# A new order of tile work in a fused shift-and-binary-convolution stage, with three of four sign pieces on GpSimd

## The reference

```python
x = x + shift(_gn(x))       # layer 0: offsets dy, dx (0 to 28) from the mean features; the image moved by them, zeros outside
x = x + conv3x3(sign(_gn(x)), sum of sign(W)) + b      # layer 1: SAME padding
x = x + spectral(_gn(x))    # layer 2: DCT along y, DFT along x, 32 x 32 modes mixed, back, relu with a 1x1 product
x = x + spectral(_gn(x))    # layer 3: the same with other weights
```

## Time and profile before

| | us |
|---|---|
| median of 3 runs | 4056.27 |
| the profiled execution, its own time | 4058.18 |
| its span, first to last instruction | 4056.4 |
| the first stage, until the last piece of its spectrum is copied | about 2203 |
| first `add_conv` of image 1 to that of image 14 | 1702.3 (13 periods of 130.9) |
| busy in the span: PE, DVE, ACT, POOL | 3117.6 (77%), 2755.7 (68%), 1483.0 (37%), 36.9 (1%) |
| bytes moved, mean rate | 808.65 MB, 199 GB/s |

### The profile page before, as it was taken

The page is one execution under the profiler, slowest core; times in us unless marked ns, Lnnn a source line. Parts: engine busy times, 40 slices in busy tenths (PEclk is TensorE's granted clock), DMA queues, the critical chain, the costliest instruction groups (busy, mean ns, idle before and its releaser), DMA issues. The chain is left out here.

```text
span 4056.4 us, 58465 instructions
## 1 busy us (share of the span) xinstructions
PE 3117.6 (77%) x17264; PEld 1421.0 (35%) x17264; DVE 2755.7 (68%) x3864; ACT 1483.0 (37%) x2708; POOL 36.9 (1%) x23
## 2 busy tenths in 40 slices
PE   0277877787877877778786579988998964799997
PEld 0133333333333333233333533333333324344443
DVE  3777665766577656766651557777677744599998
ACT  3455653655455544565433422222222214000000
POOL 0000000000000000000000000000000001000000
PEclk9987886888788877788887589999999976799998
DMA  4666544654466445655433475655665516799998
GB/s 144 176 183 199 160 155 130 203 169 150 131 188 203 141 130 163 203 160 155 139 111 107 93 293 213 251 214 205 240 247 201 219 61 125 270 379 387 390 385 305
DMA packets 272195, 808.65 MB, mean 199 GB/s; under 512 B 85466, under 2 KB 119774, under 8 KB 261108
## 3 DMA queue, kind: packets, MB, share of 16 engines
q1 hardware_dynamic: 212948, 488.15, 37.9%
q10 hardware_dynamic: 58368, 316.72, 20.3%
q0 software_dynamic: 608, 0.63, 0.1%
HBM read 479.39 MB, written 329.56 MB: 199 GB/s over the span
## 5 line engine op out<-in xcount | busy, mean ns | idle before, releaser
L817 DVE SCALAR_TENSOR_TENSOR A_image<-A_cps,A_cbias,A_image 128x896 f32<-128x896 f32 x224 | 257.3, 1149 | 492.0 <-PE A_cps L455 491.7
L1371 ACT ACTIVATE B_junk<-B_im,B_nk 128x896 bf16<-128x896 f32 x224 | 232.8, 1039 | 724.9 <-DVE B_im L1429 585.1
L455 PE MATMUL A_cps<-A_sign,A_cfull 128*128 128x448 bf16 x1344 | 448.9, 421 | 11.3 <-issue 11.3
L595 ACT ACTIVATE A_tout<-A_aps 112x512 f32<-112x512 f32 x448 | 244.5, 589 | 531.9 <-PE A_aps L482 531.5
L482 PE MATMUL A_aps<-a_k_ident,A_image 128*112 128x128 f32 x1792 | 313.5, 331 | 140.5 <-DVE A_image L817 124.5
L1622 PE MATMUL C_ring<-C_im,C_wnorm 128*128 128x448 f32 x896 | 388.9, 573 | 23.0 <-DVE C_ubuf L1679 17.8
L460 PE MATMUL A_cps<-A_sign,A_cedge 32*32 32x448 bf16 x1344 | 405.3, 415 | 0.0
L462 PE MATMUL A_cps<-A_sign,A_cedge 32*32 32x448 bf16 x1344 | 404.9, 414 | 0.0
L1317 PE MATMUL B_ring<-B_im,B_wnorm 128*128 128x448 f32 x896 | 384.5, 570 | 7.7 <-DVE B_wnorm L1400 5.5
L496 PE MATMUL A_vps<-A_tout,a_k_dctj 112*32 112x512 f32 x896 | 289.3, 780 | 118.3 <-ACT A_tout L595 118.2
L1289 PE MATMUL B_ring<-B_rout,iB_k_rowf 128*64 128x512 f32 x896 | 282.2, 714 | 118.3 <-DVE B_rout L1422 118.3
(11 more groups left out here) (193 smaller groups left out, 3436.5 us busy)
## 6 DMA issues: line engine op xcount, KB each, us to landing
A_rin<-in_x SPq DMA_DIRECT2D x2016, 112.0 KB, 2.4
x2s<-A_image ACTq DMA_DIRECT2D x112, 896.0 KB, 4.6
B_im<-x2s SPq DMA_DIRECT2D x112, 896.0 KB, 9.7
x3s<-B_im ACTq DMA_DIRECT2D x112, 896.0 KB
C_im<-x3s SPq DMA_DIRECT2D x112, 896.0 KB, 11.9
out<-C_rout ACTq DMA_DIRECT2D x192, 256.0 KB
out<-C_rout ACTq DMA_DIRECT2D x192, 192.0 KB
out<-C_rout ACTq DMA_DIRECT2D x64, 128.0 KB
```

What stands on the lines that cost most here:

```text
L455: return nc.tensor.matmul(banks[:, s, 0:LPN], cfull[:, tap, :], lines(n, s, slice(0, P), 0, tap), start=(tap == 0), stop=(tap == 2), skip_ ...
```

## The change

- `X_BY` and `S_BY` are new: x tiles in slots 0 to 9, s tiles in slots 0 to 12, one or two of each a slot. The x tiles of slot 0, and with them the wait for the buffer of image b-1, stand ahead of `add_conv(0)` on DVE.
- The second half of the spectrum is spread over slots 0 to 4, two items a slot, one ahead of `turn_back` and one behind it; each `forward_rows` comes after the next piece of other work. It writes into a bank `wps` of its own, which also holds the small averages (`mps` becomes its first 16 columns). `specout` is a tile of its own. SP stores it in slot 6.
- Step 4 of the statistics moves on PE from slot 12 ahead of unit 13's work to slot 13 behind unit 13; steps 0 to 3 of the next image's group norm move to slots 11 to 14; the second half of step 2 on DVE becomes a part called step 4, behind the signs. `root` moves to slot 13, `lower` to slot 14 ahead of the last square.
- DVE makes only piece 0 of the signs. POOL makes pieces 1 to 3: piece 1 once `nk_ready` says that the threshold is there and all units of the image before are convolved, pieces 2 and 3 once the units that read the buffer are. PE and `add_conv` wait for the new semaphore `sign_rest`; so does `centered`.
- Two [128 x 1] products of DVE (L736, L855) become `tensor_scalar`.

```diff
-        X_BY = [0, 2, 5, 7, 9, 11, 13, 14, 15, 16, 16, 16, 16, 16, 16, 16]
-        S_BY = [0, 0, 0, 1, 2, 3, 4, 6, 8, 10, 13, 16, 16, 16, 16, 16]
+        X_BY = [2, 4, 5, 7, 8, 10, 11, 13, 14, 16, 16, 16, 16, 16, 16, 16]
+        S_BY = [1, 2, 4, 5, 6, 7, 9, 10, 11, 12, 14, 15, 16, 16, 16, 16]
...
-                    if has_tail and s == 4:
+                    if has_tail and s == 6:
                         store_spec(b - 1)
...
-                pe.wait_ge(sign_full, 4 * b + piece_of(n) + 1)
+                if piece_of(n) == 0:
+                    pe.wait_ge(sign_full, b + 1)
+                else:
+                    pe.wait_ge(sign_rest, 3 * b + piece_of(n))
...
                     if has_v and s < UNITS:
                         conv(b, s)
+                    if has_tail and s < 5:
+                        spectrum(b - 1, 2 * s, ring_base(b))
+                    if has_s and s == 13:
+                        statistics(b, 4)
                     if has_v and s >= 3 and s % 2 == 1:
                         forward_cols(b, q, (s - 3) // 2)
                     if has_v and 1 <= s <= UNITS:
                         turn_back(b, q, s - 1)
-                    if has_tail and s < 2:
-                        spectrum(b - 1, 4 * s, ring_base(b))
-                    if has_s and s == 12:
-                        statistics(b, 4)
-                    if has_x and s >= 13:
-                        statistics(b + 1, s - 12)
+                    if has_tail and s < 4:
+                        spectrum(b - 1, 2 * s + 1, ring_base(b))
+                    if has_x and s in (11, 12, 14):
+                        statistics(b + 1, {11: 1, 12: 2, 14: 3}[s])
...
+                    if has_tail and s < 4:
+                        copy_cols(b - 1, 2 * s, ring_base(b) + ring_t(2 * s))
                     if has_v and 1 <= s <= UNITS:
                         copy_back(b, q, s - 1)
-                    if has_tail and s < 2:
-                        for k in range(4 * s, 4 * s + 4):
-                            copy_cols(b - 1, k, ring_base(b) + ring_t(k))
-                    if has_tail and s == 2:
+                    if has_tail and s < 4:
+                        copy_cols(b - 1, 2 * s + 1, ring_base(b) + ring_t(2 * s + 1))
+                    if has_tail and s == 5:
                         copy_spec(b - 1)
+                    if has_x and s == 13:
+                        root(b + 1)
...
+                    if has_x and s == 14:
+                        lower(b + 1, (q + 2) % 3)
                     if has_v and 1 <= s <= UNITS:
                         square(b, q, s - 1)
...
-                    if has_v and s < UNITS:
+                    if has_v and 0 < s < UNITS:
                         add_conv(b, q, s)
...
-                    if has_v and s in (1, 4, 7):
-                        signs(q, (s + 2) // 3)
+                    if has_x and s in (11, 12):
+                        statistics(b + 1, s - 11, far)
...
                         turn_x(far, k, x_at(k) % RING, tile_loaded(b, x_at(k)))
+                    if has_v and s == 0:
+                        add_conv(b, q, s)
...
                     if has_s and s == 13:
+                        if has_v:
+                            dve.wait_ge(sign_rest, 3 * (b + 1))
                         centered(b, nxt)
-                        if has_v:
-                            dve.wait_ge(conv_full, UNITS * (b + 1))
-                        signs(nxt, 0)
                     if has_x and s == 13:
-                        statistics(b + 1, 0, far)
+                        statistics(b + 1, 2, far)
+                    if has_s and s == 13:
+                        signs(nxt)
+                    if has_x and s == 13:
+                        statistics(b + 1, 4, far)
                     if has_x and s == 14:
-                        statistics(b + 1, 1, far)
-                    if has_x and s == 15:
-                        statistics(b + 1, 2, far)
                         statistics(b + 1, 3, far)
...
+            def signs(b, q, c):
+                if c == 1:
+                    pool.wait_ge(nk_ready, b + 1)
+                    if not isinstance(b, int) or b > 0:
+                        pool.wait_ge(conv_full, UNITS * b)
+                else:
+                    pool.wait_ge(conv_full, UNITS * b + PIECES[c - 1])
+                rows, lines = sg[c % 2], lps(q).rearrange("p l (j s) -> p l s j", s=2)
+                lo, hi = 2 * PIECES[c], 2 * PIECES[c + 1]
+                pool.sem_inc(pool_seen, 1)
+                for edge, lp, s in ((0, lo - 1, 1), (2 * (hi - lo) + 1, hi, 0)):
+                    if lp < 2 * UNITS:
+                        nc.gpsimd.tensor_scalar(rows[:, edge, 2:2 + SIZE], lines[:, lp, s, :], m1[:], 2.0, ALU.is_ge, ALU.mult)
+                    else:
+                        nc.gpsimd.memset(rows[:, edge, 2:2 + SIZE], 1.0)
+                for s in range(2):
+                    last = nc.gpsimd.tensor_scalar(rows[:, 1 + s:1 + s + 2 * (hi - lo):2, 2:2 + SIZE], lines[:, lo:hi, s, :],
+                                                   m1[:], 2.0, ALU.is_ge, ALU.mult)
+                last.then_inc(sign_rest, 1)
```

101 lines of the change are left out of this document (58 added, 43 removed).

## The result

The changed kernel takes 3847.1 us (median of 4 runs, 3835.3 to 3855.2) against 4056.0 of the kernel before (4 runs, 4053.5 to 4059.1): ratio 0.9482, 95% interval 0.9456 to 0.9508. The gain is 209 us where 340 were forecast. The direction and the wide range (3570 to 3880) held; the forecast's own range (3640 to 3800) did not, and the time missed the predicted 3716 by 131 us. The profiled execution took 3845.86 us with a span of 3844.1, 212 us less than the span before.

What follows compares the result with a forecast made beforehand. No engine saturated: PE and ACT, then DVE, take turns in the first stage's 130.9 us period. 82.4 + 6 + 7 + 4 + 4.5 + 3 = 106.9; 13 x 24.0 = 312, with the ends 340: 3716 us, own range 3640 to 3800, wide 3570 to 3880.

Steps and rivals of the forecast that it cites:

- the port term: DVE instructions held by GpSimd at the shared SBUF port: 4.5 us a period, with up to 17 as upper bound.
- PE and ACT in slots 0 to 3: ACT's near 9 us a slot against DVE's 6 to 7.6 costs 4 us a period, bounds 1 and 8.
- SP and DMA: DVE's waits for tile loads, with SP's queue held by the spectrum's store: 7 us a period, bounds 3 and 14.
- The end of the body: From unit 13's add to the next unit 0's add, 14 to 15 us, of which DVE waits 6.
- Loop ends: Loop returns and late starts between bodies: 3 us a period kept, from 3.7 before.
- DVE's occupied time: DVE's period less its waits, 89.4 us, falls by 7.0 of signs to 82.4, the base of the sum.
- Signs: Pieces 1 to 3 leaving DVE: 7.6 us of instructions an image, about 7.0 off its occupied time.
- Its cover: GpSimd's pieces have time before their use, piece 2 some 18 us, so even 35 us of work stays hidden from PE.
- Loads become the bound: Rival, 15%: tile loads in the first stage set a period of 115 us, time 3830.
- The port costs everything: Rival, 8%: GpSimd's 17 us fall wholly on DVE, period 119.4 us, time 3893.
- Slower: Rival, 7%: GpSimd's sign rate sets the period; at 15 ns an element 154.6 us, time 4366.
- everything overlaps: Rival, 10%: no port collisions, smaller load, ACT and end terms; period 96.4 us, time 3575.

Runs made afterwards that it cites:

- the run with no pieces: The changed kernel with GpSimd's large sign instructions left out and two elements written per edge line, so nobody makes pieces 1 to 3: 3740.1 us, ratio 0.9216.
- small ones: The changed kernel with each large GpSimd sign instruction cut into one per line of 224 elements: 3757.3 us, ratio 0.9241.
- the two moves: New order with all signs on DVE, plus the spectrum's store in slot 13 and some x tiles put off to later slots: 3683.1 us, ratio 0.9074.
- the best version: The changed kernel with GpSimd's signs in single lines, the spectrum's store in slot 13 and some x tiles put off: 3662.3 us, ratio 0.9012.

## Why the prediction was right and wrong

**The sum against the runs.** Without the port term the forecast was 82.4 + 6 + 7 + 4 + 3 = 102.4 us a period; the run with no pieces has 110.5. With it the forecast was 106.9, and 116.1 came. So 8.1 of the 9.2 us that are missing have nothing to do with GpSimd, and 13 x 9.2 = 120 of the 131 us are explained by the period. The time lay in the wide range, but the period lay outside of the forecast's own, 101 to 113.

- *PE and ACT in slots 0 to 3, 4 us (bounds 1 and 8)*: mis-sized. Slots 1 to 3 take 30.8 us for 21.0 of DVE's work: 9.8, outside of the bounds. I counted ACT's instructions in a slot, but not their order: two tiles' sums and squares stand ahead of the copy that PE waits for, and the clock, costed at nothing with "its cover", is part of the price exactly there, since PE ends the wait in these slots and, in the rows shown, fell to 1.2 GHz behind its own wait.
- *SP and DMA, 7 us (bounds 3 and 14)*: DVE's waits for loads are (73.4 + 40.0) / 13 = 8.7 us a period in the run with no pieces, in slots 5 to 9. The mechanism, the spectrum's store holding the loads back in slot 6, was named and is right; moving it gave 3.0 back.
- *PE in slots 11 and 12*: no term in the sum. DVE waits there for PE's convolutions for another 3.3 us a period in that run; with the loads' 8.7 this is more than the 10.8 by which slots 5 to 12 (53.7 us) exceed DVE's work (42.9). Why PE is late there was not tried.
- *The end of the body, 6 us of waits*: too large. Forecast T + 14 to 15, 12.7 without pieces, so about 4, which makes up for part of the terms that were too small.
- *Loop ends, 3 us*: the medians of the slots in that run add up to 106.9, so 3.6.
- *DVE's occupied time, 89.4 - 7.0*: the arithmetic holds (73.6 of work in slots 0 to 12 and some 9 at the end), but the base was the wrong thing to subtract from. It makes every freed microsecond count in full. Slots 1 to 3 and most of 5 to 9 have waits for PE or loads, and there DVE's signs cost next to nothing: 1.1 of 7.0. This is the error of the kind that a larger margin doesn't cure: the term was counted before it was asked what ends the slot.
- *Signs*: for the same reason this part of the change is worth little here even with a GpSimd that hardly disturbs: 1.1 us a period with the pieces left out, 2.1 with small ones (111.6 to 109.5), 1.7 behind the two moves.

**GpSimd.** *Its rate*: 17 us an image forecast, 35 as upper end, 40 measured: out of the bounds. *Its cover*: right, even so. *What it does to DVE*: 4.5 forecast, 5.6 measured net, which looks good and is partly luck: the gross lengthening is some 18, from the masks and from three tiny instructions that I had not counted as candidates, while the large adds, which I had, were spared (1181 for 1152). Two errors, a gross price taken four times too small and waits of DVE, not thought of, that soak up two thirds of it, met in the middle. The rule of the Trainium skill that spoke against the change (SBUF — State Buffer, "Who interferes with whom") was worth more than the weight of half a term that I gave it: it named who can be hit, which the trace of before could not. Even so, the estimate of nearly 8 that I drew from it is less than half of the gross 18, and more than the 5.6 that show.

**The ends.** Image 14 came out right (92.6 for 93) by luck: it was put down to PE alone, but takes 81.6 us with no pieces, so 11.0 of the 92.6 are GpSimd's. Image 15 was nearly right (9.3 for 8). Image 0 was not: 98 forecast, 108.7 measured, 92.9 with no pieces, so the miss is GpSimd's. There DVE has few waits to hide in: its busy time grew from 78.4 to 97.6 us, and 15.8 of these 19.2 show.

**The rivals.** "Loads become the bound" gave 3830, the nearest time, by another mechanism: DVE waits for loads 5.5 us a period, not over 15, and the best version moves the same tiles in a body 11 us shorter at a DMA share of 0.67. "The port costs everything" (119.4 a period, 17 us of blocking) has the right culprit and a price near the gross one of 18, but two thirds of it are covered. "Slower", by GpSimd's rate, needed 12.7 ns an element; it has 3.2 to 3.7. "No change" and "everything overlaps" are out.

**What would show it.** Right: DVE's signs only in slot 13; no `add_conv` waiting for POOL; the end of the body under 20 us (19.6, just). Nearly: the waits for PE (6.9 for "under 6"). Missed: 1509 us between images 1 and 14 for 1390; POOL at work 40 us a period for 10 to 25; a DMA share of 0.7 throughout, as the end of the body has 0.15; and the clock, 0.83 for "over 0.85". The mark for the port was put on L832, which hardly moved: the gauge was fixed to the wrong instruction.
